# Experts two at a time on 128 rows, and v evicted and transposed once: one change to a fused window-attention and mixture-of-experts kernel

## The reference, cut to what matters

```python
qkv = jnp.einsum('oi,bihw->bohw', qkv_w, xh)          # 32 channels each of q, k, v
lepe = depthwise_3x3(v)
attn = softmax(q * scale @ k^T + bias)                # 16 tokens of a window, per head
out = attn @ v + lepe
...
router_probs = softmax(x @ router_w + router_b)       # 8 experts
top_p, top_i = top_k(router_probs, 2);  top_p /= sum(top_p)
expert_out = einsum('bnd,edc->bnec', x, expert_w) + expert_b
y = sum over the two chosen experts of top_p * expert_out
```

## Time and profile before

| | |
|---|---|
| median of 3 runs | 3960.85 us |
| lowest and highest | 3948.16, 3964.89 us |
| the profiled execution | 3955.5 us, of which the span of the records is 3953.7 us |
| TensorE busy | 3575.8 us (90%) |
| VectorE busy | 3195.4 us (81%) |
| ScalarE busy | 2298.3 us (58%) |
| GpSimd busy (its DMA issues count) | 1532.2 us (39%) |
| DMA engines, mean busy share | 2 to 3 tenths |

### The profile page before, as it was taken

One profiled execution on the slowest core, in us unless ns is written; L12 is line 12 of the kernel. 1 busy time (PEld: TensorE's weight loads), 2 busy tenths in 40 slices (PEclk: granted clock), 3 DMA queues, 4 the chain that ended last, 5 costly groups with the idle time before them and its releaser, 6 DMA issues.

```text
span 3953.7 us, 204756 instructions
## 1 busy us (share of the span) xinstructions
PE 3575.8 (90%) x83621; PEld 2122.4 (54%) x83621; DVE 3195.4 (81%) x7043; ACT 2298.3 (58%) x4708; POOL 1532.2 (39%) x2698
## 2 busy tenths in 40 slices
PE   3899999998999989999999999999899999999986
PEld 1655555555555555555555555555555555555542
DVE  3888888887888878888788878888888888888873
ACT  3766656565656555666566556666566666666640
POOL 2544444343434433434343434444344443444420
PEclk8999999999999999999999999999999999999986
DMA  2222222222222222222222222222222222222220
GB/s 38 74 79 74 72 75 71 76 71 72 74 73 73 76 69 69 80 73 74 64 77 71 75 68 76 70 77 71 74 69 77 70 77 70 78 71 77 70 57 22
DMA packets 216196, 279.22 MB, mean 71 GB/s; under 512 B 79872, under 2 KB 190512, under 8 KB 215216
## 3 DMA queue, kind: packets, MB, share of 16 engines
q1 hardware_dynamic: 141488, 152.22, 14.5%
q0 software_dynamic: 73728, 113.39, 10.3%
HBM read 95.46 MB, written 56.62 MB: 38 GB/s over the span
## 4 chain that ended last, share of the span: by engine, by line
PE 67%; DVE 13%; ACT 9%; issue 8%; SPq 1%; DVEq 1%; DMA 0%; ACTq 0%
PE bank L611 20%; PE bank L527 13%; PE bank L543 10%; DVE v2t L943 5%; PE bank L566 4%; PE bank L624 4%; PE bank L518 3%; PE bank L616 3%; PE bank L583 3%; DVE gx L899 3%; ACT row_inv L683 2%; PE bank L638 2%; ACT row_inv L681 2%; PE bank L643 2%; DVE yn L953 2%
## 5 line engine op out<-in xcount | busy, mean ns | idle before, releaser
L477 POOL DMA_DIRECT2D kx<-k_sb x1536 | 736.9, 487 | 1074.1 <-ACT k_sb L733 1062.0
L611 PEld LDWEIGHTS bank<-probT,vx 128*32 128x32 f32 x36864 | 831.2, 193 | 217.6 <-issue 204.6
L611 PE MATMUL bank<-probT,vx 128*32 128x16 f32 x36864 | 888.8, 235 | 6.3 <-issue 5.6
L527 PE MATMUL bank<-gx,expert_sb 128*128 128x384 f32 x1536 | 717.1, 549 | 196.0 <-DVE gx L899 196.0
L899 DVE TENSOR_TENSOR gx<-bank,yn 128x384 f32<-128x384 f32 x768 | 423.1, 551 | 538.4 <-PE bank L518 536.2
L543 PEld LDWEIGHTS bank<-kx,qx 32*32 32x32 f32 x36864 | 562.0, 107 | 323.5 <-issue 320.4
L543 PE MATMUL bank<-kx,qx 32*32 32x64 f32 x36864 | 663.1, 220 | 54.6 <-issue 45.0
L486 POOL DMA_DIRECT2D vx<-v2t x768 | 382.0, 504 | 637.3 <-PE bank L616 525.4
L495 POOL TENSOR_TENSOR lepe_p<-lepe_p,tap_sb 128x384 f32<-128x384 f32 x384 | 403.8, 1051 | 574.7 <-ACT tap_sb L748 570.7
L910 DVE SCALAR_TENSOR_TENSOR lepe<-vpad,lepe_sb,lepe 128x384 f32<-128x384 f32 x960 | 589.7, 614 | 0.0
L710 ACT ACTIVATE prob<-prob 128x512 f32<-128x512 f32 x576 | 363.7, 631 | 231.7 <-DVE prob L930 231.7
(11 more groups left out here) (100 smaller groups left out, 4641.9 us busy)
## 6 DMA issues: line engine op xcount, KB each, us to landing
vx<-v2t POOLq DMA_DIRECT2D x768, 96.0 KB, 2.8
kx<-k_sb POOLq DMA_DIRECT2D x1536, 24.0 KB
z<-fin SPq DMA_DIRECT2D x1344, 24.0 KB
xs<-in_x SPq DMA_DIRECT2D x96, 192.0 KB
xt<-in_x SPq DMA_DIRECT2D x192, 96.0 KB
z0t<-z SPq DMA_DIRECT2D x192, 96.0 KB
out_y<-y_out SPq DMA_DIRECT2D x192, 96.0 KB, 2.5
xs<-in_x SPq DMA_DIRECT2D x96, 139.5 KB
```

The source lines that it names most:

```text
L477: pool.dma_start(kx[to + m:to + C:4, r % 2, m, :], k_sb[at + m:at + C:4, r % 2, :])\
L527: MM(bank_f[:, 0:SPX], expert_sb[:, e, :], gx[:, e % 2, :], start=False, stop=(e == E - 1))\
L611: last = MM(bank_o[32 * c:32 * c + 32, at * TOK:(at + 1) * TOK], vx[:, kr % 2, :, at * 4 + c], probT[:, kr % 2, at, c * TOK:(c + 1) * TOK] ...
```

## The change

Experts. The weights of experts 2i and 2i+1 are stacked on the 128 rows as [128, 64], with no zeros. A gate matmul now spreads the gate of expert 2i over rows 0 to 63 and that of expert 2i+1 over rows 64 to 127, for one half (strip) of the tile; there are still eight a tile. `gateT` and `expert_sel` have 128 rows, those from 48 up zero. `gx` is the product with `yn_pair`, in which both row halves hold the same strip of `yn`; four DMAs per tile on GpSimd's queue make it, in a new stage `pair_yn` (lag 31). `gx` is a ring of four. At odd e TensorE does two matmuls of 64 columns of weights, one for each half, into `bank_f` rows 0 to 63 and 64 to 127; at even e it does none.

v. ScalarE evicts v once, unmasked, into `v_sb`. VectorE transposes its 384 columns. `spread_v` (lag now 8) issues 16 DMAs a strip, each placing 16 partitions by 4 runs of 48 elements into a `vx` cleared once, so that the zeros between them stay.

```diff
-    spread_k=4, turn_v=5, place_bias=6, spread_v=7, score=7, shift=8,
+    spread_k=4, turn_v=5, place_bias=6, spread_v=8, score=7, shift=8,
+    pair_yn=31, gap_exp=33, turn_gates=34, experts=35, tile_out=39)
...
-        v2 = sb("v2", [128, 2, WIN, 2, TOK])
-        v2t = sb("v2t", [128, 2, 8, WIN, 4])
+        v_sb = sb("v_sb", [128, 2, SPX])
+        vt = sb("vt", [128, 2, 8, WIN // 2, 4])
-        vx = sb("vx", [128, 2, 32, WIN * 4])
+        vx = sb("vx", [128, 2, 32, 2, WIN // 2 * 4])
-        gateT = sb("gateT", [3 * GE, 2, SPX], BF16)
-        gx = sb("gx", [128, 2, SPX])
+        gateT = sb("gateT", [128, 2, SPX], BF16)
+        yn_pair = sb("yn_pair", [128, 2, 2, SPX])
+        gx = sb("gx", [128, 4, SPX])
...
                 if st := s.strip("spread_v"):
                     k, r = st
-                    wait_alone(pool, v2t_made, k + 1)
+                    wait_alone(pool, vt_made, k + 1)
                     if s.later(r, 2):
                         wait_alone(pool, pv_made, (k - 1) * UNITS)
                     for g in range(4):
-                        rows = slice(32 * g, 32 * g + 32)
-                        pool.dma_start(vx[rows, r % 2, g * 8:g * 8 + 8, :].rearrange("p q n -> p (q n)"),
-                                     v2t[rows, r % 2, :, :, :].rearrange("p q n k -> p (q n k)")).then_inc(v_spread[r % 2], 16)
+                        for x in range(2):
+                            for odd in range(2):
+                                to, at = g * CH + x * TOK, g * CH + odd * TOK
+                                pool.dma_start(vx[to:to + TOK, r % 2, g * 8 + x:g * 8 + 8:2, odd, :],
+                                               vt[at:at + TOK, r % 2, x::2, :, :].rearrange("p h n k -> p h (n k)"))\
+                                    .then_inc(v_spread[r % 2], 16)
+                if ti := s.tile("pair_yn"):
+                    k, r = ti
+                    wait_alone(pool, yn_made, k + 1)
+                    if s.later(r, 2):
+                        wait_alone(pool, gx_made, (k - 1) * E)
+                    for half in range(2):
+                        for to in range(2):
+                            pool.dma_start(yn_pair[to * C:(to + 1) * C, r % 2, half, :],
+                                           yn[half * C:(half + 1) * C, r % 2, :]).then_inc(yn_paired[r % 2], 16)
...
                     pe.wait_ge(gx_made, k * E + (e + 1))
-                    MM(bank_f[:, 0:SPX], expert_sb[:, e, :], gx[:, e % 2, :], start=False, stop=(e == E - 1))\
-                        .then_inc(expert_made, 1)
+                    if e % 2:
+                        for half in range(2):
+                            last = MM(bank_f[half * C:(half + 1) * C, 0:SPX], expert_sb[:, e // 2, :],
+                                      gx[:, (e - 1 + half) % 4, :], start=False, stop=(e == E - 1),
+                                      skip_group_check=True)
+                        last.then_inc(expert_made, 1)
...
-                    for x in range(2):
-                        S.activation(v2[:, r % 2, :, x, :].rearrange("p n (r w) -> p n r w", w=SP),
-                                     windows(bank_p[0][:, 0:SPX]), ACT.Copy,
-                                     scale=const("mask_v")[:, x:x + 1]).then_inc(v2_made, 1)
+                    S.activation(by_window(v_sb[:, r % 2, :]), windows(bank_p[0][:, 0:SPX]), ACT.Copy).then_inc(v_copied, 1)
...
                     dve.wait_ge(gate_spread, k * E + (e + 1))
-                    if r * E + e >= 2:
-                        dve.wait_ge(expert_made, k * E + e - 1)
-                    V.tensor_tensor(gx[:, e % 2, :], bank_g[:, 0:SPX], yn[:, r % 2, :], ALU.mult).then_inc(gx_made, 1)
+                    if e == 0:
+                        dve.wait_ge(yn_paired[r % 2], (k // 2 + 1) * 64)
+                    if r * E + e >= 4:
+                        dve.wait_ge(expert_made, k * (E // 2) + e // 2 - 1)
+                    V.tensor_tensor(gx[:, e % 4, :], bank_g[:, 0:SPX], yn_pair[:, r % 2, e % 2, :], ALU.mult)\
+                        .then_inc(gx_made, 1)
...
-                    V.transpose(v2t[:, r % 2, :, :, :].rearrange("p q n k -> p n k q"), v2[:, r % 2, :, :, :].rearrange("p n x i -> p (n x i)")).then_inc(v2t_made, 1)
+                    V.transpose(vt[:, r % 2, :, :, :].rearrange("p q n k -> p n q k"), v_sb[:, r % 2, :]).then_inc(vt_made, 1)
```

More of the change, by code:

```diff
@@ L157, in _constants @@
         "mask_q": ((p[:, None] // 16 & 1) == np.arange(2)[None, :]) * HD ** -0.5,
-        "mask_v": (p[:, None] & 1) == np.arange(2)[None, :],
         "ones": (p[:, None] // 32 == np.arange(32)[None, :] // 8) & (p[:, None] // TOK % 2 == np.arange(32)[None, :] % 2),
         "mask_b": (p[:, None] // TOK % 4) == p[None, :4],
-        "expert_sel": np.stack([(p[:, None] % E == e) & (p[:, None] // E % 2 == p[None, :] // C)
-                                & (p[:, None] < 3 * GE) for e in range(E)], axis=1).reshape(128, E * 128),
+        "expert_sel": np.stack([(p[:, None] % E == 2 * (i // 2) + p[None, :] // C) & (p[:, None] // E % 2 == i % 2)
+                                & (p[:, None] < 3 * GE) for i in range(E)], axis=1).reshape(128, E * 128),
         "rank": np.tile(E - np.arange(E), (128, 1)),
@@ L210, in metaformer_block @@
         router_bias = sb("router_bias", [GE, 1])
[L211 to L215, removed]
+        expert_sb = sb("expert_sb", [128, E // 2, C])
+        expert_sel = sb("expert_sel", [128, E, 128], BF16)
+        ebias_sb = sb("ebias_sb", [128, 128])
+        ebias_rest = sb("ebias_rest", [128, 2, 128])
+        ebias_part = sb("ebias_part", [128, 3, 128], BF16)
         ident_bf = sb("ident_bf", [128, 128], BF16)
@@ L281, in metaformer_block @@
             sem("logit_saved"), sem("gap_made"), sem("gap_exp"), sem("gate_step"))
+        yn_paired = sems("yn_paired")
         gates_made, gateT_made, gateT_saved = sem("gates_made"), sem("gateT_made"), sem("gateT_saved")
@@ L313, in metaformer_block @@
         MM = nc.tensor.matmul
-        N_CONST_MADE = 6
+        N_CONST_MADE = 7
         N_SPREAD_CLEARED = 2
         N_WEIGHT_DMAS = 1 + 3 + 16 + 2 + 12 + 4 + 6
-        X_DMAS, Z_DMAS, TILE_DMAS, K_DMAS, V_DMAS = 5, 11, 7, 8, 4
+        X_DMAS, Z_DMAS, TILE_DMAS, K_DMAS, V_DMAS = 5, 11, 7, 8, 16
         block = ctx.enter_context(nc.Block())
@@ L354, in _ @@
                     sp.dma_start(router_sb[rows, half * E:(half + 1) * E], router_w).then_inc(const_loaded, 16)
-                    sp.dma_start(expert_sb[rows, :, rows], expert_w.rearrange("e d c -> d e c")).then_inc(const_loaded, 16)
+                    sp.dma_start(expert_sb[rows, :, :], expert_w.rearrange("(p e) d c -> e d p c", e=2)[half])\
+                        .then_inc(const_loaded, 16)
                     for part in range(3):
@@ L579, in slot @@
                     pe.wait_ge(v_saved, k + 1)
-                    wait_alone(pe, v2_made, (k + 1) * 2)
+                    wait_alone(pe, v_copied, k + 1)
                     for g in range(4):
@@ L651, in slot @@
                     for part in range(3):
-                        MM(bank_f[:, 0:SPX], ebias_part[:, part, :], gateT[:, r % 2, :], start=(part == 0), stop=False)
+                        MM(bank_f[:, 0:SPX], ebias_part[:, part, :], gateT[:, r % 2, :], start=(part == 0), stop=(part == 2))
                     spread_gate(k, r, 0)
@@ L686, in slot @@
                     act.wait_ge(gateT_made, k + 1)
-                    S.activation(gateT[:, r % 2, :], bank_p[0][0:3 * GE, 0:SPX], ACT.Copy).then_inc(gateT_saved, 1)
+                    S.activation(gateT[0:3 * GE, r % 2, :], bank_p[0][0:3 * GE, 0:SPX], ACT.Copy).then_inc(gateT_saved, 1)
                 if st := s.strip("variance"):
@@ L771, in _ @@
             V.memset(vpad[:, :], 0.0).then_inc(const_made, 1)
+            V.memset(gateT[:, :, :].rearrange("p a n -> p (a n)"), 0.0).then_inc(const_made, 1)
             dve.wait_ge(const_loaded, 16 * N_WEIGHT_DMAS)
-            step = [4]
+            step = [3]
             def chained(ins):
@@ L788, in _ @@
                     some = heads_of(2, g).rearrange("p (h a b y) -> p b h a y", h=HD, a=2, b=2)[:, b]
-                    V.tensor_copy(wv[:, g * CH + 16 * b:g * CH + 16 * b + 16].rearrange("p (a h y) -> p h a y", a=2, y=2), some)
+                    V.tensor_copy(wv[:, g * CH:(g + 1) * CH].rearrange("p (h y b a) -> p b h a y", h=HD, y=2, b=2)[:, b], some)
                     last = V.tensor_copy(wo[:, 64 * b:64 * b + 64].rearrange("p (a g h y) -> p g h a y", a=2, g=4, y=2)[:, g], some)
@@ L922, in slot @@
                     k, r = yt
-                    dve.wait_ge(expert_made, (k + 1) * E)
+                    dve.wait_ge(expert_made, (k + 1) * (E // 2))
                     if s.later(r, 2):
```

17 lines of the change are left out of this document (8 added, 9 removed).

## The result

The changed kernel takes 3803.9 us (median of 4 runs, 3796.4 to 3805.5), against 3962.9 for the kernel before on the same chip. The ratio is 0.960, with a 95% interval of 0.957 to 0.963: faster by 4.0%. The forecast was 3695 with a range of 3615 to 3810, so the time lies in the range, near its slow end, and outside the 3640 to 3740 of the case called likeliest. It lies where rival 1 put it (3750 to 3835).

A forecast was written before the change was run, and what follows sets the result against it. PE was taken to bound a 39.04 us tile, DVE 6 us behind. Gains of 3.17 us less 0.05 for each of 4 pairs and 0.2 spill gave 2.77, times 96 tiles 266 us: 3695 us, range 3615 to 3810.

The forecast's parts named there:

- the case called likeliest: The forecast itself, for the whole kernel's time: 3640 to 3740 us, chance 0.57.
- rival 1: On DVE: the moved GpSimd adds take its slack, partly where PE waits for gx; 3750 to 3835 us, chance 0.17.
- PE and the pairs: On PE: a pair costs 0.88 us; removing even experts' matmuls gains 0.84 at expert 3, 0.81 at expert 5.
- rival 2: On PE: column halves run one after the other, a pair costs 1.68 us, time 3965, no change; chance 0.07.
- v: On DVE: halving the 1520 ns transpose to 0.76 us gains 0.76 us each at experts 1 and 7.
- GpSimd's own load: On POOL: 30.1 us a tile against a period of about 36, 0.504 us a DMA; nothing waits for it.
- Rival 3: POOL becomes the bound once a DMA costs over 0.68 us; at 0.9 the time is 4480 us; chance 0.10.
- The packets: On the DMA engines: 245760 packets at 88 ns each, 34% of the engines in place of 10%, hidden.
- The spill of 0.2 us a tile: On DVE: moved adds collide with two-input instructions, two collisions of 0.85 us, mostly covered by slack; 0.2 us lost a tile.
- The sign that was to tell of this: In the profile after: DVE's taps and adds growing over 0.1 us on the mean would show the prediction wrong.
- 285 us were forecast before any spill: The tile's gains of 3.17 us less 4 x 0.05 for pairs: 2.97 a tile without spill, over 96 tiles.
- The lower granted clock: On PE: the prediction is wrong if a less dense PE gets its lower clock for longer than a few slices.

The follow-up runs named there:

- the adds read nothing: Changed kernel with each GpSimd add replaced by a memset of similar length that reads no SBUF, leaving out two of nine taps: 3613.1 us, 0.913.
- The later tile: Changed kernel with every mixture-of-experts stage from tile_sum on 6 slots later, giving the trip through memory 9 slots instead of 3: 3772.6 us, 0.954.
- adds first: Changed kernel with GpSimd's adds written ahead of the v DMAs in its slot instead of behind them: 3704.6 us, 0.937.
- the timed adds: Changed kernel, adds ahead of the v DMAs, each started after DVE's row maximum of the slot; 16 v DMAs split 10 and 6 over two slots: 3650.5 us, 0.922.
- the timed adds and the later tile: Changed kernel with GpSimd's adds placed by DVE's progress and the mixture of experts 6 slots later: 3585.9 us, 0.907.
- all v DMAs behind both adds: Changed kernel with adds ahead of the v DMAs and spread_v in slot lag 9 instead of 8: 3680.7 us, 0.929.

## Why the prediction came out as it did

**PE and the pairs: right.** 2.53, 1.07, 1.17 and 2.36 us from place 0 to 1 were measured for 2.56, 1.07, 1.04 and 2.26 worked out. A pair costs 0.80, under the 0.88 taken; rival 2 is out (by the prediction's own terms it stood for 4002 us, or 3983 without the spill, and not for 3996 and 3965). The Trainium skill, "TensorEngine Tiling (Array Packing)", Key Properties, says that a change of the tiling mode drains the engine. No drain stands out here, but none is excluded: the pair's 0.80 is 0.06 above the 0.74 between two full-array matmuls, and the staggered start of the halves can be that too.

At experts 1 and 7 the good numbers are in part luck. DVE's path from the divide to the product became 0.89 and 0.88 us shorter and not 0.76, and the divide began 0.10 and 0.22 us later after place 0, so that 0.79 and 0.66 were left.

**v: right in kind.** The transpose is 0.568 us, not 0.76, near the lower bound of 0.53 that the `turn_p` row gave. I halved a number whose excess over that row was not in proportion to the columns.

**GpSimd's own load: right.** 515 and 526 ns a DMA for the 504 taken, busy 30.4 us of a 37.5 us tile for the 30.1 worked out, no PE wait on `vx`. DVE waited for `lepe_p` six times, 14.7 us in all, where none was expected. Rival 3 is out by a wide margin (0.68). The packets were wrong, which cost nothing: q0 shows 165888 and 12.0% for the 245760 and 34% worked out, so the 64 packets and 88 ns each don't hold for the new DMAs.

**The spill of 0.2 us a tile: this step failed.** The prediction saw the collision and put it down as a small spill, because the adds would fall "in slots with slack". The lock cost 75 us before and 191 after (185 by the ratios, as the two runs belong to different groups); what the change added is 116 us, or 1.2 us a tile, six times the term. Two things were wrong in it. It counted only DVE's slack to expert 0, but a blocked `y` or `gate_tmp` stands in the chain to `tile_sum`, the gates and PE's turned gates (114 us of waits for `gate_part`, 7 before). Not all of these waits are the lock's: 66 remain where the adds read nothing, and 5 where the tile is later too. And it took two collisions of 0.85 a tile, 1.7 us of DVE, where DVE's 259 us are 2.7 a tile. Rival 1, with its 3750 to 3835, was this lock at the right size, but in another place: it put the loss where PE waits for `gx`, and those waits fell, from 196 to 171 us. The range took in a part of rival 1; that the time lies in it is due to that, and not to the term.

The sign that was to tell of this (taps and adds longer by more than 0.1 us on the mean) didn't show: the taps grew by 0.09 and the adds by 0.06. `fin`, `y` and two products of 48 columns, which it didn't name, grew by 0.16 to 0.49.

**The trip through memory was missing.** No step of the prediction asked which fixed latency spans a fixed number of slots. The later tile gave back 31 us in the change (3803.9 to 3772.6; 21 by the ratios, whose intervals leave 5 to 38), 32 where the adds read nothing (3613.1 to 3581.6; 26), 40 with adds first (47) and 65 with the timed adds (60).

**The sum without both.** 285 us were forecast before any spill. Without reading adds the change is worth 3879.9 - 3613.1 = 267 us, and 3879.9 - 3581.6 = 298 with the longer trip as well. So the other terms hold together to some 20 us, and the miss of 109 us is mostly the lock's 116 less its 19 forecast, and some of the trip. They hold in part because errors offset: with the transpose at its measured 0.57 us the same sum would have been 0.4 a tile higher, and that was not seen.

The lower granted clock was named as what could go wrong. In the stretch from 250 to 3400 us it was 0.99 before, 0.96 after, 0.98 with adds first, and 0.99 with the adds that read nothing and with the timed adds and the later tile. It doesn't simply follow the time: with all v DMAs behind both adds it was 0.96, in a kernel 24 us faster than adds first. How much of the 109 us it carries was not measured by itself, but the pages say where to look: for the same 83621 matmuls PE was busy 3275 us after the change and 3187 with the memsets. So some 87 of the 191 us that the lock costs passed inside PE's own matmuls, at a mean granted clock of 0.94 against 0.97, and not in its waits; in the kernel before it was 11 of 75 (3576 and 3565, at 0.97 and 0.98). This is an estimate, since the ends of matmuls are modelled in a page.

## What to carry to other kernels

Before moving a GpSimd compute instruction that reads SBUF, even by moving DMAs ahead of it, list which VectorE instructions with inputs in SBUF will lie beside it, those with two above all; its price is the lengthening of those and of the chains behind them, and an otherwise idle GpSimd gives no cover. Tie such an instruction to VectorE's progress (start it when a stretch of PSUM-reading work begins) rather than to its data's readiness. And when a change shortens the slots of a software pipeline, look for the latencies in microseconds that span a fixed number of slots, stores and reloads above all, and give them slots to spare (six more were tried here).

## What the hardware showed

- A VectorE instruction with two SBUF inputs doesn't run beside a GpSimd add: 0.55 to 0.61 us became 1.6 to 2.2. Even a product of 48 columns (0.20 us alone) took 0.99 beside an add, and one of six columns 1.28 on the mean (0.16). A GpSimd memset of the same length did nothing to them: taps 595 ns. The Trainium skill, "SBUF — State Buffer", "SBUF: two separate sides", has this rule, for two SBUF inputs against a GpSimd instruction that reads SBUF, and the runs here agree with it. Transposes of one input kept their length (701 to 703 and 568 ns in every order of the adds), but a `TENSOR_SCALAR` of one input did not (0.16 to 0.51); no run here settles what tells the two apart. One thing isn't explained by the times as recorded: `y` began at 2039.64 and ran 2.17 us, though the first add's record starts only at 2040.37, when `y` alone would have been over; the spans on GpSimd are rough.
- 16 DMAs of 64 runs of 192 bytes cost GpSimd 515 ns each to issue, next to 504 for 32 rows of 3072 bytes. So issue time on that queue hardly depended on the pattern here.
- In the same kernel the granted clock fell to 1.2 GHz after PE waits: where PE stood 2.06 us for `y`, the score's 64 MATMULs took 1.93 us, and 1.10 in the next slot:

```profile
2005.52 1.29 PE L648 MATMUL bank<-y,const_sb 128*128 128x384 f32 x2 [2.06 <-DVE y L982]
2006.74 1.93 PE L561 MATMUL bank<-kx,qx 32*32 32x64 f32 x64
...
2013.72 1.10 PE L561 MATMUL bank<-kx,qx 32*32 32x64 f32 x64
```

The windows of the same moment: length, busy of PE, PEld, DVE, ACT and POOL, granted clock, DMA share, GB/s. The clock is 0.50 in the stretch behind the idle one:

```profile
2003.40:2006.00 2.60, 0.55 (x3) 0.30 (x2) 2.56 (x6) 1.37 (x3) 2.52 (x5) 0.98 0.15 56
2006.00:2008.50 2.50, 2.50 (x66) 1.69 (x64) 2.43 (x9) 0.87 (x2) 2.50 (x6) 0.50 0.31 95
```
